# Low parts of a chunk's products and down weights made in the middle of a five-instruction split on GpSimd

## The chip, the cores and the metric

The kernel runs on one NeuronCore of a Trainium2 chip. The metric is the device time of one execution in microseconds (us), the median over several executions. The engines are TensorE (PE in the profile; its weight loads PEld), VectorE (DVE), ScalarE (ACT), GpSimd (POOL) and SyncE (SP, which here only issues DMAs). Each engine works through its own list of instructions in order; they meet through semaphores.

## The reference, cut to what matters

```python
xn = layernorm(x)                                    # x: 8 x 256 tokens x 128
qkv = xn @ Wqkv + bqkv                               # 16 heads of width 8
q = q * cos + rotate_half(q) * sin                   # k in the same way
probs = softmax(q @ k.T / sqrt(8));  attn = (probs @ v) @ Wout + bout
s = sigmoid(xn @ gate_w + gate_b)                    # 16 experts
values, experts = top_k(s, 2);  values /= values.sum()
mlp(x, wg, wu, wd) = (silu(x @ wg) * (x @ wu)) @ wd  # inner width 64
ffn = xn + mlp(xn, shared) + sum(values * mlp(xn, experts))
out = x + attn + ffn
```

Everything is computed in full for every expert; the routing weights, zero for all but two experts of a token, multiply the products before the down projection.

## The kernel before, in words

The 8 sequences are worked in 4 groups of two (512 token columns a group). Two streams of work are woven into each other by a hand-written order of **blocks** from -6 to 33. All engines run the same loop over the blocks, each doing its share of a block.

**The expert stream.** The shared MLP and the 16 experts make 9 chunks a group (the shared one with 64 rows, then two experts a chunk with 128), 36 in all. Block b starts chunk n = b + 6 and carries on with chunk m = b + 5. For a chunk, PE makes the up products in the banks FA and FB (three matmuls each: high weights times high input, low times high, high times low, lines 374 to 376). ACT takes the tanh (`th`, L673), DVE forms `th` (L895) and the product `gu` (L876). GpSimd multiplies `gu` by the routing weights `wbc` (L986). ACT writes the rounded high part `hid_hi` (L694), GpSimd the low part `hid_lo` = `gu` - `hid_hi` (L1002), and PE multiplies both by the down weights into the bank Y, one block later. The down weights have a low part `wd_lo` too, which GpSimd makes chunk by chunk while m is below 9 (L969). The weights `wbc` of a chunk come by two DMAs issued by SP (`load_route`, L336) ahead of their use.

**The attention stream.** The rotated q and k of a sequence are split into three bfloat16 parts by five dependent instructions (`split_stage`): stage 0 adds the two halves of the rotation (L253), stage 1 casts part 0 (L257), stage 2 takes the rest (L259), stage 3 casts part 1 (L261), stage 4 makes part 2 (L262). There are 14 such splits on GpSimd (in the blocks of the table `SPLIT_BLOCK`); the first is in block -6, where no chunk is yet under way, and the others in -5, -2, -1, 0, 2, 6, 7, 9, 10, 14, 16, 17 and 18. When both splits of a sequence are done, SP writes the parts to DRAM (six DMAs, `scratch`, L303) and reads them back in another layout (`load_hats`, L318, into `q_hat` and `k_hat`). PE makes scores for the row maxima from them (S1, L487), DVE reduces these (`mx`, L886), GpSimd splits the maxima (`md`, L947 to L951), and four blocks after the first scores PE makes the scores again with the maxima in extra rows (S2, L501). ACT exponentiates them (`probs`, L661), and PE multiplies by the values (PV, L515), which waits for all four exponentials of the block before.

**The order on each queue around the change.** SP's list is fixed: the parts and hats of sequence 0, two `wbc` chunks, the parts and hats of sequence 1, then from block -6 on the rest, beginning with the `wbc` of the third, fourth and fifth chunk with a routing weight that is not loaded yet. ACT's order in a block is: exponential 0; tanh, exponential 1 and the copies of other banks; exponential 2, then `hid_hi`; and where a new group starts, the copies `xT_hi` and `xT` of the transposed input (L592, L595) before exponential 3. GpSimd's order in a block is: the maxima (`md`), `gu`, `xT_lo` (the low part of a new group's input, L961), the residual (L957), the split of this block, `wd_lo`, `hid_lo`, and the final sum (L1010).

The lines that the change touches are `split_batch` and its call in GpSimd's loop.

Of the kernel before, what the change touches and what calls it, by code (L numbers as in the profile page):

```python
# [33 lines left out]
CHLEAD = 6  # L34
ROUTE_STAGES = 7
SPLIT_STAGES = 5
PART_STAGES = (1, 3, 4)
FIRST, LAST = -CHLEAD, NBLK + 1

# [21 lines left out]
SPLIT_BLOCK = {  # L61
# [4 lines left out]
}  # L66
# [13 lines left out]
def early_b(blk):  # L80

    return [(kind, of) for kind, blocks in EARLY_B.items() for of, at in blocks.items() if at == blk]


def negated_half(blk):

    return blk // 2 + 1 if blk % 2 == 0 and blk // 2 + 1 in range(2 * B) else None
# [20 lines left out]
def bank_uses():  # L108

    a = {("G1", 0): 0, ("G2a", 0): 1, ("G3a", 0): 2}  # L110
    b = {("G2b", 0): 0, ("G3b", 0): 1, ("G4b", 0): 2}
    s = {}
    for blk in range(FIRST, LAST + 1):
        n, q = blk + CHLEAD, blk + LEAD
        if n < NCHUNKS:
            a["hg", n] = len(a)
        for what in late_a(blk):
            a[what] = len(a)
        for what in early_b(blk):
            b[what] = len(b)  # L120
        if n < NCHUNKS:
            b["hu", n] = len(b)
        for i in range(NQ):
            if 0 <= q < NBLK:
                s["max", q * NQ + i] = len(s)
            if i == 0 and transposed_half(blk) is not None:
                s["M", transposed_half(blk)] = len(s)
    return a, b, s


def layer_kernel(nc, x, wqk, wv, bias, wout, gate_w, gate_b, swg, swu, swd, ewg, ewu, ewd,
# [5 lines left out]
    A_USE, B_USE, S_USE = bank_uses()  # L137
# [7 lines left out]
    with ctx:  # L145
# [6 lines left out]
        def sem(name):  # L152
            return ctx.enter_context(nc.semaphore(name))
# [55 lines left out]
        stage = wbc[:, 1].rearrange("p c t -> p (c t)")  # L209
# [23 lines left out]
        fa_ready, fa_read, fb_ready, fb_read = sem("fa_ready"), sem("fa_read"), sem("fb_ready"), sem("fb_read")  # L233
# [6 lines left out]
        def chunk_group(n):  # L240
            return n // NCH, n % NCH
# [5 lines left out]
        def split_stage(engine, queue, stage, w, g, slot):  # L247


            cols = slice(slot * T, (slot + 1) * T)  # L250
            whole, left, part = rope[:, w, 0, cols], rest[:, w, cols], [parts[:, w, k, cols] for k in range(PARTS)]
            if stage == 0:
                return engine.tensor_tensor(whole, whole, rope[:, w, 1, cols], ALU.add)  # L253
            if stage == 1:
                if g:
                    queue.wait_ge(scratch_done[slot], 16 * WRITES * g)
                return engine.tensor_scalar(part[0], whole, 1.0, 1.0, ALU.mult, ALU.mult)  # L257
            if stage == 2:
                return engine.tensor_tensor(left, whole, part[0], ALU.subtract)  # L259
            if stage == 3:  # L260
                return engine.tensor_scalar(part[1], left, 1.0, 1.0, ALU.mult, ALU.mult)  # L261
            return engine.tensor_tensor(part[2], left, part[1], ALU.subtract)  # L262
# [642 lines left out]
        def _(pool):  # L905
            steps = [0]

            def after(instruction):

                steps[0] += 1  # L910
                instruction.then_inc(pool_step, 1)
                pool.wait_ge(pool_step, steps[0])
# [9 lines left out]
            for k, (w, hi, lo) in enumerate(((wg_sb, wg_hi, wg_lo), (wu_sb, wu_hi, wu_lo))):  # L922
                pool.wait_ge(up_hi_ready, k + 1)
                nc.gpsimd.tensor_tensor(lo[:], w, hi[:].bitcast(f32), ALU.subtract).then_inc(up_split, 1)
            def split_batch(w, g, slot):
                kind = ("G2", "G3")[w]
                pool.wait_ge(fa_read, A_USE[kind + "a", g] + 1)
                pool.wait_ge(fb_read, B_USE[kind + "b", g] + 1)
                for stage in range(SPLIT_STAGES):
                    instruction = split_stage(nc.gpsimd, pool, stage, w, g, slot)  # L930
                    if stage not in PART_STAGES:
                        after(instruction)
                        continue
                    instruction.then_inc(parts_done[slot], 1)
                    if stage < SPLIT_STAGES - 1:
                        pool.wait_ge(parts_done[slot], PARTS * (2 * g + w) + PART_STAGES.index(stage) + 1)

# [35 lines left out]
            for blk in range(FIRST, LAST + 1):  # L973
                n = blk + CHLEAD
                m = n - 1
                if negated_half(blk) is not None:
                    negate_maxima(negated_half(blk))
                if 0 <= m < NCHUNKS:
                    g, c = chunk_group(m)
                    pool.wait_ge(fb_read, B_USE["hu", m] + 1)  # L980
                    if c == 0:
                        nc.gpsimd.tensor_scalar(gu[0:I, m % 2, :], gu[0:I, m % 2, :], 0.5, 1.0,
                                                ALU.mult, ALU.mult).then_inc(gu_weighted, 1)
                    else:
                        pool.wait_ge(wbc_ld[c - 1], 32 * (g + 1))
                        nc.gpsimd.tensor_tensor(gu[:, m % 2, :], gu[:, m % 2, :], wbc[:, g % 2, c - 1, :],  # L986
                                                ALU.mult).then_inc(gu_weighted, 1)
                for kind, g in late_a(blk):
                    if kind == "G1":
                        xt_low(g)  # L990
                for g in range(G):
                    if blk == RESIDUAL_BLOCK[g]:
                        residual(g)
                for (g, w, slot), at in SPLIT_BLOCK.items():
                    if blk == at:
                        split_batch(w, g, slot)
                if 0 <= m < NCH:
                    down_low(m)
                if 0 <= m < NCHUNKS:
                    rows = I if m % NCH == 0 else P  # L1000
                    pool.wait_ge(hid_hi_ready, m + 1)
                    nc.gpsimd.tensor_tensor(hid_lo[0:rows, m % 2, :], gu[0:rows, m % 2, :],  # L1002
                                            hid_hi[0:rows, m % 2, :].bitcast(f32), ALU.subtract).then_inc(hid_ready, 1)
                for kind, g in early_b(blk):
                    if kind == "O2":
                        pool.wait_ge(fb_read, B_USE[kind, g] + 1)
                        flat = resid[:, g % 2].rearrange("p t c -> p (t c)")

                        pool.wait_ge(fa_read, A_USE["O1", min(GB * g + 1, B - 2)] + 1)
                        nc.gpsimd.tensor_tensor(flat, flat, y_tok[:], ALU.add).then_inc(o_ready, 1)  # L1010
# [61 lines left out]
```

## Time and profile before

| | us |
|---|---|
| median of the runs | 248.81 |
| lowest and highest of 3 runs | 248.80, 249.73 |
| the profiled execution | 249.88 |
| its span, from the first to the last instruction | 248.1 |
| PE busy in the span | 215.0 |
| DVE busy | 182.7 |
| POOL busy | 174.3 |
| ACT busy | 141.9 |

The profiled execution is 1.07 us above the median. Busy time is a sum over stages with different limits; which engine sets the pace has to be read from each stretch of the trace. Times in the rows below are from the start of the span.

### The profile page before, as it was taken

The numbers are of one execution on the slowest core, as the hardware profiler recorded it, in microseconds if no ns is written. First come the engines' busy times: TensorE is split into PE (matmuls) and PEld (weight loads), VectorE is DVE, ScalarE is ACT, GpSimd is POOL, SyncE is SP. The second block draws the span as 40 slices with busy tenths as digits, with TensorE's granted clock in tenths as the row PEclk, the third lists the DMA queues.
The fourth block names the chain that finished last, engine by engine and source line by source line (L and its number), as shares of the span: only waits on it lengthen the run. The fifth ranks groups of instructions, "written<-read, shape, count | busy, mean of one in ns | idle before, by whom it ended". The sixth has DMA issues, their size and how long they took to land.

```text
span 248.1 us, 4856 instructions
## 1 busy us (share of the span) xinstructions
PE 215.0 (87%) x1612; PEld 140.9 (57%) x1612; DVE 182.7 (74%) x400; ACT 141.9 (57%) x266; POOL 174.3 (70%) x254
## 2 busy tenths in 40 slices
PE   0474399869798999999998999999999999999973
PEld 0342255546465566666674566666766667675541
DVE  5987349958777687999976787998688878774301
ACT  2554322314565766676567476666676767667761
POOL 9184297599998757996966577879886774658622
PEclk9997769979999999999999999999999999999999
DMA  7925344520160276130565150405524640311101
GB/s 223 366 45 168 95 145 139 169 88 0 46 180 21 80 196 155 44 106 10 154 193 166 50 148 26 124 5 174 153 64 127 194 141 19 82 56 35 44 3 42
DMA packets 35954, 26.53 MB, mean 107 GB/s; under 512 B 4237, under 2 KB 30157, under 8 KB 35917
## 3 DMA queue, kind: packets, MB, share of 16 engines
q1 hardware_dynamic: 35224, 25.30, 34.4%
q10 hardware_dynamic: 704, 0.92, 1.0%
q8 instruction: 13, 0.21, 0.4%
q14 instruction: 13, 0.10, 0.1%
HBM read 18.53 MB, written 7.47 MB: 105 GB/s over the span
## 4 chain that ended last, share of the span: by engine, by line
PE 52%; POOL 19%; DVE 11%; issue 6%; DMA 4%; ACT 4%; SPq 3%; POOLq 0%; DVEq 0%; ACTq 0%
PE PV L515 9%; PE S2b L501 5%; POOL hid_lo L1002 4%; PE S2a L501 4%; PE S1a L487 3%; PE S1b L487 3%; POOL gu L986 3%; PE Y L374 3%; PE FB L374 3%; PE FB L376 2%; PE FB L375 2%; PE FA L374 2%; PE Y L375 2%; PE Y L376 2%; PE FA L376 2%
## 5 line engine op out<-in xcount | busy, mean ns | idle before, releaser
L1002 POOL TENSOR_TENSOR hid_lo<-gu,hid_hi 128x512 fp32r<-128x512 f32 (+1 forms) x36 | 46.1, 1281 | 25.5 <-ACT hid_hi L694 25.5
L661 ACT ACTIVATE probs<-S2b 128x512 f32<-128x512 f32 x64 | 38.2, 596 | 30.1 <-PE S2b L501 29.9
L886 DVE TENSOR_REDUCE mx<-S1a 128x2 f32<-128x512 f32 x65 | 44.4, 684 | 10.4 <-PE S1a L487 10.4
L886 DVE TENSOR_REDUCE mx<-S1b 128x2 f32<-128x512 f32 x63 | 43.0, 683 | 7.7 <-PE S1b L487 7.6
L661 ACT ACTIVATE probs<-S2a 128x512 f32<-128x512 f32 x64 | 38.4, 599 | 12.7 <-PE S2a L501 10.6
L986 POOL TENSOR_TENSOR gu<-gu,wbc 128x512 f32<-128x512 f32 x32 | 41.1, 1285 | 6.0 <-DVE gu L876 4.2
L515 PE MATMUL PV<-probs,vx 128*32 128x256 f32 x512 | 34.9, 384 | 1.7 <-ACT probs L661 1.7
L694 ACT ACTIVATE hid_hi<-gu 128x512 fp32r<-128x512 f32 (+1 forms) x36 | 22.7, 632 | 21.3 <-POOL gu L986 19.4
L895 DVE SCALAR_TENSOR_TENSOR th<-th,FA 128x512 f32<-128x512 f32 (+1 forms) x36 | 24.6, 682 | 10.8 <-ACT th L673 10.2
L673 ACT ACTIVATE th<-FA 128x512 f32<-128x512 f32 (+1 forms) x36 | 21.5, 598 | 17.0 <-PE FA L376 16.6
L876 DVE TENSOR_TENSOR gu<-FB,th 128x512 f32<-128x512 f32 (+1 forms) x36 | 24.6, 683 | 8.4 <-PE FB L376 8.3
L487 PE MATMUL S1a<-k_hat,q_hat 96*128 96x256 bf16 x130 | 25.3, 275 | 1.1 <-DVE mx L886 1.1
L501 PE MATMUL S2a<-q_hat,k_hat 102*128 102x256 bf16 x128 | 24.9, 276 | 0.2 <-ACT probs L661 0.2
L501 PE MATMUL S2b<-q_hat,k_hat 102*128 102x256 bf16 x128 | 25.0, 277 | 0.0
L487 PE MATMUL S1b<-k_hat,q_hat 96*128 96x256 bf16 x126 | 24.5, 275 | 0.4 <-DVE mx L886 0.2
L515 PEld LDWEIGHTS PV<-probs,vx 128*32 128x32 f32 x512 | 15.6, 109 | 11.8 <-ACT probs L661 6.9
L374 PE MATMUL Y<-hid_hi,wd_hi 128*128 128x512 f32 (+1 forms) x36 | 17.7, 492 | 4.3 <-POOL hid_lo L1002 4.3
L374 PE MATMUL FB<-xT_hi,wu_hi 128*128 128x512 f32 (+1 forms) x36 | 17.7, 492 | 3.8 <-ACT sig L613 3.6
L501 PEld LDWEIGHTS S2b<-q_hat,k_hat 102*128 102x128 bf16 x128 | 8.6, 98 | 18.1 <-issue 15.9
L374 PE MATMUL FA<-xT_hi,wg_hi 128*128 128x512 f32 (+1 forms) x36 | 17.6, 488 | 1.1 <-ACT xT L595 0.9
L501 PEld LDWEIGHTS S2a<-q_hat,k_hat 102*128 102x128 bf16 x128 | 9.5, 98 | 11.1 <-issue 7.1
L487 PEld LDWEIGHTS S1a<-k_hat,q_hat 96*128 96x128 bf16 x130 | 11.9, 99 | 5.4 <-DVE mx L886 2.5
(129 smaller groups left out, 435.3 us busy)
## 6 DMA issues: line engine op xcount, KB each, us to landing
wbc<-route_w SPq DMA_DIRECT2D x64, 128.0 KB, 3.0
q_hat<-q_parts SPq DMA_DIRECT2D x32, 96.0 KB, 2.6
k_hat<-k_parts SPq DMA_DIRECT2D x32, 96.0 KB, 2.7
k_parts<-parts SPq DMA_DIRECT2D x8, 192.0 KB, 2.1
q_parts<-parts SPq DMA_DIRECT2D x8, 192.0 KB, 2.2
x_sb<-in_x SPq DMA_DIRECT2D x4, 256.0 KB, 4.1
q_parts<-parts SPq DMA_DIRECT2D x8, 128.0 KB, 2.1
k_parts<-parts SPq DMA_DIRECT2D x8, 128.0 KB, 2.1
```

The source lines that it names most:

```text
L374: nc.tensor.matmul(bank, w_hi, m_hi, start=start, stop=False)
L487: last = nc.tensor.matmul(bank[:, t * T:(t + 1) * T], q_hat[0:MROW, slot, pair, t * P:(t + 1) * P], k_hat[0:MROW, slot, pair, r, :], start ...
L501: last = nc.tensor.matmul(S2[head % 2][:, s * T:(s + 1) * T], k_hat[0:KALL, slot, pair, r, s * P:(s + 1) * P], q_hat[0:KALL, slot, pair, : ...
L515: last = nc.tensor.matmul(PV[32 * j:32 * j + 32, hg * T:(hg + 1) * T], vx[:, (b // GB) % 2, SB * (b % GB) + s, r, NQ * hg + j, :], probs[: ...
L661: nc.scalar.activation(probs[:, head % (2 * NQ), :], S2[head % 2][:], ACT.Exp, scale=SCALE).then_inc(exp_done, 1)
L673: nc.scalar.activation(th[0:rows, n % 2, :], FA[0:rows, :], ACT.Tanh, scale=0.5).then_inc(th_ready, 1)
L694: nc.scalar.activation(hid_hi[0:rows, (n - 1) % 2, :], gu[0:rows, (n - 1) % 2, :], ACT.Copy).then_inc(hid_hi_ready, 1)
L876: nc.vector.tensor_tensor(gu[0:rows, m % 2, :], FB[0:rows, :], th[0:rows, m % 2, :], ALU.mult).then_inc(fb_read, 1)
L886: nc.vector.tensor_reduce(mx[:, (q // QB) % 2, (q // 2) % 2, :, q % 2, i], S1[use % 2][:].rearrange("p (t s) -> p t s", t=SB), axis=AX.X, ...
L895: nc.vector.scalar_tensor_tensor(th[0:rows, n % 2, :], th[0:rows, n % 2, :], 1.0, FA[0:rows, :], ALU.add, ALU.mult).then_inc(fa_read, 1)
L986: nc.gpsimd.tensor_tensor(gu[:, m % 2, :], gu[:, m % 2, :], wbc[:, g % 2, c - 1, :], ALU.mult).then_inc(gu_weighted, 1)
L1002: nc.gpsimd.tensor_tensor(hid_lo[0:rows, m % 2, :], gu[0:rows, m % 2, :], hid_hi[0:rows, m % 2, :].bitcast(f32), ALU.subtract).then_inc(hi ...
```

## The change

A split's five instructions are no longer issued in one piece. `split_batch` takes a first and an end stage and is called twice in a block: once for stages 0 and 1 where the whole split stood, and once for stages 2 to 4 behind `wd_lo` and `hid_lo`. The waits for the split's inputs stay in front of stage 0. The wait for stage 1 to be done, which stage 2 needs, stays behind stage 1 and so now stands in front of `wd_lo` or `hid_lo`.

```diff
+SPLIT_PAUSE = 2
...
-            def split_batch(w, g, slot):
+            def split_batch(w, g, slot, first, end):
                 kind = ("G2", "G3")[w]
-                pool.wait_ge(fa_read, A_USE[kind + "a", g] + 1)
-                pool.wait_ge(fb_read, B_USE[kind + "b", g] + 1)
-                for stage in range(SPLIT_STAGES):
+                if first == 0:
+                    pool.wait_ge(fa_read, A_USE[kind + "a", g] + 1)
+                    pool.wait_ge(fb_read, B_USE[kind + "b", g] + 1)
+                for stage in range(first, end):
                     instruction = split_stage(nc.gpsimd, pool, stage, w, g, slot)
...
                 for (g, w, slot), at in SPLIT_BLOCK.items():
                     if blk == at:
-                        split_batch(w, g, slot)
+                        split_batch(w, g, slot, 0, SPLIT_PAUSE)
                 if 0 <= m < NCH:
                     down_low(m)
                 if 0 <= m < NCHUNKS:
...
                     nc.gpsimd.tensor_tensor(hid_lo[0:rows, m % 2, :], gu[0:rows, m % 2, :],
                                             hid_hi[0:rows, m % 2, :].bitcast(f32), ALU.subtract).then_inc(hid_ready, 1)
+                for (g, w, slot), at in SPLIT_BLOCK.items():
+                    if blk == at:
+                        split_batch(w, g, slot, SPLIT_PAUSE, SPLIT_STAGES)
```

The number of instructions is the same on every engine (257 rows on GpSimd in both), and no other engine's list changes. Line numbers of the changed kernel are one or two higher here than in the kernel before.

On GpSimd in block -5, the second split, which completes sequence 1, with the first chunk (m = 0). Before:

```order
L961 TENSOR_TENSOR xT_lo<-xT,xT_hi 128x512
L253 TENSOR_TENSOR rope<-rope 128x256
L257 TENSOR_SCALAR parts<-rope 128x256
L259 TENSOR_TENSOR rest<-rope,parts 128x256
L261 TENSOR_SCALAR parts<-rest 128x256
L262 TENSOR_TENSOR parts<-rest,parts 128x256
L969 TENSOR_TENSOR wd_lo<-wbc,wd_hi 64x128
L1002 TENSOR_TENSOR hid_lo<-gu,hid_hi 64x512
L986 TENSOR_TENSOR gu<-gu,wbc 128x512
```

The same place in the changed kernel:

```order
L963 TENSOR_TENSOR xT_lo<-xT,xT_hi 128x512
L254 TENSOR_TENSOR rope<-rope 128x256
L258 TENSOR_SCALAR parts<-rope 128x256
L971 TENSOR_TENSOR wd_lo<-wbc,wd_hi 64x128
L1004 TENSOR_TENSOR hid_lo<-gu,hid_hi 64x512
L260 TENSOR_TENSOR rest<-rope,parts 128x256
L262 TENSOR_SCALAR parts<-rest 128x256
L263 TENSOR_TENSOR parts<-rest,parts 128x256
L988 TENSOR_TENSOR gu<-gu,wbc 128x512
```

`wd_lo` and `hid_lo` moved ahead of the last three instructions of the split, and so the last `parts`, for which SP waits, moved behind them; the next `gu` stands where it stood.

On GpSimd in block 0 (chunk m = 5), followed by block 1's `gu`. Before:

```order
L986 TENSOR_TENSOR gu<-gu,wbc 128x512
L253 TENSOR_TENSOR rope<-rope 128x256
L257 TENSOR_SCALAR parts<-rope 128x256
L259 TENSOR_TENSOR rest<-rope,parts 128x256
L261 TENSOR_SCALAR parts<-rest 128x256
L262 TENSOR_TENSOR parts<-rest,parts 128x256
L969 TENSOR_TENSOR wd_lo<-wbc,wd_hi 128x128
L1002 TENSOR_TENSOR hid_lo<-gu,hid_hi 128x512
L986 TENSOR_TENSOR gu<-gu,wbc 128x512
```

The same place in the changed kernel:

```order
L988 TENSOR_TENSOR gu<-gu,wbc 128x512
L254 TENSOR_TENSOR rope<-rope 128x256
L258 TENSOR_SCALAR parts<-rope 128x256
L971 TENSOR_TENSOR wd_lo<-wbc,wd_hi 128x128
L1004 TENSOR_TENSOR hid_lo<-gu,hid_hi 128x512
L260 TENSOR_TENSOR rest<-rope,parts 128x256
L262 TENSOR_SCALAR parts<-rest 128x256
L263 TENSOR_TENSOR parts<-rest,parts 128x256
L988 TENSOR_TENSOR gu<-gu,wbc 128x512
```

Here too `hid_lo` stands three instructions nearer to its own `gu`, and the following `gu` has the same instructions ahead of it as before.

## Rows read from the trace of the kernel before

**Rows 1.** The page: the chain that ended last, share of the span by engine.

```profile
PE 52%; POOL 19%; DVE 11%; issue 6%; DMA 4%; ACT 4%; SPq 3%; POOLq 0%; DVEq 0%; ACTq 0%
```

**Rows 2.** Who waited for whom, whole span: us in total, times, longest.

```profile
PE Y L374 <- POOL hid_lo L1002: 4.3, 4, 2.2
```

**Rows 3.** POOL's timeline in block -5: start, us, engine, line, operation, tiles.

```profile
32.48 0.67 POOL L259 TENSOR_TENSOR rest<-rope,parts 128x256 f32<-128x256 f32 x1
...
33.73 0.67 POOL L262 TENSOR_TENSOR parts<-rest,parts 128x256 bf16<-128x256 f32 x1
34.36 0.45 POOL L969 TENSOR_TENSOR wd_lo<-wbc,wd_hi 64x128 fp32r<-64x128 f32 x1
34.78 1.26 POOL L1002 TENSOR_TENSOR hid_lo<-gu,hid_hi 64x512 fp32r<-64x512 f32 x1
36.00 1.28 POOL L986 TENSOR_TENSOR gu<-gu,wbc 128x512 f32<-128x512 f32 x1
```

**Rows 4.** The chain that ended last, 34 to 47 us: start, us, what.

```profile
34.42 0.35 SPq L303
...
40.15 1.37 SPq L318
...
44.00 2.86 DMA wbc<-route_w
```

**Rows 5.** SP's loads of k_hat: duration ns min/median/max, first and last start us.

```profile
L318 SPq DMA_DIRECT2D k_hat<-k_parts x32: 333/443/1372, 22.6 to 203.1; - x32
```

**Rows 6.** POOL's timeline, block -2: start, us, and idle before with its releaser.

```profile
47.00 1.29 POOL L986 TENSOR_TENSOR gu<-gu,wbc 128x512 f32<-128x512 f32 x1 [1.77 <-DMA wbc<-route_w]
...
49.56 0.68 POOL L259 TENSOR_TENSOR rest<-rope,parts 128x256 f32<-128x256 f32 x1
```

**Rows 7.** Busy time by stretch: us, then PE, PEld, DVE, ACT, POOL (instructions), clock, DMA, GB/s.

```profile
47.00:79.00 32.00, 26.05 (x180) 16.75 (x179) 25.43 (x61) 14.83 (x28) 29.95 (x47) 0.95 0.26 77
88.00:111.00 23.00, 23.00 (x186) 15.47 (x185) 19.88 (x49) 14.61 (x29) 18.24 (x30) 1.00 0.45 123
```

**Rows 8.** PE's timeline: its three long waits for `hid_lo`, and the Y of chunk 8.

```profile
53.19 0.79 PE L374 MATMUL Y<-hid_hi,wd_hi 128*128 128x512 f32 x1 [2.22 <-POOL hid_lo L1002]
...
66.89 0.50 PE L374 MATMUL Y<-hid_hi,wd_hi 128*128 128x512 f32 x1 [1.17 <-POOL hid_lo L1002]
...
78.61 0.50 PE L374 MATMUL Y<-hid_hi,wd_hi 128*128 128x512 f32 x1 [0.77 <-POOL hid_lo L1002]
...
84.65 0.48 PE L374 MATMUL Y<-hid_hi,wd_hi 128*128 128x512 f32 x1
```

**Rows 9.** ACT's timeline: `hid_hi` of chunks 5 and 8.

```profile
61.98 0.63 ACT L694 ACTIVATE hid_hi<-gu 128x512 fp32r<-128x512 f32 x1 [1.92 <-POOL gu L986]
...
79.83 0.63 ACT L694 ACTIVATE hid_hi<-gu 128x512 fp32r<-128x512 f32 x1 [1.58 <-POOL gu L986]
```

**Rows 10.** POOL's timeline at the end of its full stretch (chunk 8).

```profile
78.53 1.28 POOL L986 TENSOR_TENSOR gu<-gu,wbc 128x512 f32<-128x512 f32 x1
81.51 1.29 POOL L961 TENSOR_TENSOR xT_lo<-xT,xT_hi 128x512 fp32r<-128x512 f32 x1 [1.71 <-ACT xT L595]
...
83.18 1.28 POOL L1002 TENSOR_TENSOR hid_lo<-gu,hid_hi 128x512 fp32r<-128x512 f32 x1
```

**Rows 11.** SP's timeline: the first DMAs behind the parts of sequence 2.

```profile
70.42 1.10 SPq L336 DMA_DIRECT2D wbc<-route_w  x2
```

**Rows 12.** Block 17: ACT's `hid_hi` and POOL's stage 2.

```profile
167.41 0.62 ACT L694 ACTIVATE hid_hi<-gu 128x512 fp32r<-128x512 f32 x1
167.44 0.67 POOL L259 TENSOR_TENSOR rest<-rope,parts 128x256 f32<-128x256 f32 x1
```

**Rows 13.** DVE's and POOL's timelines in block 16: two instructions on `wsel`, and `hid_lo`.

```profile
161.26 0.29 DVE L778 TENSOR_TENSOR wsel<-iota_sb,topf 128x128 f32<-128x128 f32 x1
162.53 1.29 POOL L1002 TENSOR_TENSOR hid_lo<-gu,hid_hi 128x512 fp32r<-128x512 f32 x1
162.65 1.32 DVE L783 TENSOR_TENSOR wsel<-wsel,tsel 128x128 f32<-128x128 f32 x1
```

## The prediction, made before the changed kernel ran

> **What bounds the kernel now.** I read the chain that ended last first. It is 52% PE, but 19% POOL [rows 1], so the question is where POOL's part lies. Followed in order of time, the chain goes through POOL's second split to 34.4 us, through SP's queue and DMAs to 47 [rows 4], through POOL again to 78.6, and from there mostly through PE to the end. The table of busy time says the same: from 47 to 79 us POOL is busy 29.95 of 32 us, the rest being short pauses between dependent instructions, and PE only 26.05; from 88 to 111 us PE is busy 23.00 of 23 and POOL 18.24 [rows 7]. So there are three stages: a start-up that hangs on SP's list, a stretch in which POOL is the bottleneck, and a long rest in which PE is. Two waits matter then. PE waits for `hid_lo` 4.3 us in four places [rows 2]; three lie in the POOL stretch, 2.22, 1.17 and 0.77 us [rows 8], which leaves 0.14 for the fourth. And POOL itself starts its full stretch late, because the `gu` at 47.00 had to wait 1.77 us for the DMA of its routing weights [rows 6].
>
> **What the change moves.** No instruction is added or taken away. In 13 blocks `hid_lo`, in the early ones with `wd_lo` ahead of it, stands in front of split stages 2 to 4. Two prices follow, both from start-to-start distances.
> `hid_lo` is released earlier by the three stages: 34.36 - 32.48 = 1.88 us [rows 3].
> The last part of the split, for which SP waits, comes later by `wd_lo` and `hid_lo`: 36.00 - 34.36 = 1.64 us [rows 3].
> The `gu` of the next block has the same work ahead of it as before and keeps its time, unless POOL now has to stand still for `hid_hi`.
>
> **Block -5, a loss on the path.** SP starts the six writes of sequence 1's parts at 34.42, right behind POOL's last part (33.73 + 0.67) [rows 3, 4]. Now `wd_lo` starts in stage 2's place at 32.48, `hid_lo` at 32.90, stage 2 at 34.12, and the last part is done at 34.40 + 1.64 = 36.04. Everything behind it in SP's list moves by 1.64 us: six writes and their landing, eight hat loads, and then the `wbc` DMA issued at 44.00 that takes 2.86 us [rows 4]. That one releases the `gu` at 47.00 [rows 6], the first instruction of POOL's full stretch. The `gu` had idled until then, so nothing hides the delay: it starts at 48.64. What `hid_lo` gains in block -5 buys nothing, since its Y is not one of the four that wait.
>
> **Blocks -2 to 3, the POOL stretch.** I see no input that would come too late for POOL, so it works on from 48.64 without a break, as from 47.00 before. `hid_hi` starts 79.83 - 78.53 = 1.30 us behind the start of its `gu` and takes 0.63 [rows 9, 10]; the new `hid_lo` stands 49.56 - 47.00 + 0.42 = 2.98 us behind it [rows 3, 6]. So every `gu` is 1.64 us late, up to the one at 78.53, which comes at 80.17.
> On PE's side the earlier `hid_lo` cancels this, and a little more: 1.64 - 1.88 = -0.24 us at each of the three waits. Y comes at about 52.9, 66.6 and 78.4. If that were all, the kernel would be no slower.
> But PE has a second tie to POOL, and the change does not loosen it. In ACT's list `hid_hi` stands in front of the last exponential of a block, and `hid_hi` waits for `gu`: 1.92 us at 61.98, 1.58 at 79.83 [rows 9]. Those exponentials are all 1.64 us late, and PE's PV products need them. So PE saves 0.24 us at a Y and loses up to 1.6 at the next PV. In block 3, which has no split to gain from, it is worst: the late `gu` makes `hid_hi`, `xT`, `xT_lo` (81.51) and `hid_lo` late by the same 1.64, and `hid_lo` ends at 83.18 + 1.28 + 1.64 = 86.10 [rows 9, 10]. The Y that started at 84.65 [rows 8], 0.2 us behind its `hid_lo`, cannot start before. PE is **1.4 us late**, and from here on PE is the bottleneck [rows 7], with nothing idle that could take the delay back.
>
> **SP's list again.** In block 0 the parts of sequence 2 come later by both shifts, 1.64 + 1.64 = 3.3 us. Behind them stand the `wbc` of chunk 8 and the hats of sequence 2. Those `wbc` loads were issued at 70.42, over 1.10 us [rows 11]; at 73.7 + 1.1 + 2.86 they land by 77.7, 2.5 us before the `gu` at 80.17. I take nothing for this.
>
> **Blocks 6 to 18, stalls of POOL.** Eight splits lie where PE is the bottleneck. There `hid_hi` can be later than stage 2 was: in block 17 it ends at 168.03 where stage 2 began at 167.44, so POOL stands still 0.59 us [rows 12], with stages 2 to 4, the maxima and the next `gu` queued behind it. That is the largest of the eight; two are zero. POOL has 4.8 us to spare in 23 [rows 7], so these do not add up. I take 0.1 us, with 0 and 0.6 (one stall that gets through) as ends. The gain there is at most the 0.14 us of PE's fourth wait.
>
> **Sum.** 1.4 + 0.1 - 0.1 = +1.4 us on the profiled execution's 249.88, which gives 251.3. That execution is 1.07 us above the median; carried to the median of 248.81 it is **250.2 us**.
>
> **A rule weighed.** Of two DVE instructions of one size, the one at 161.26 took 0.29 us and the one at 162.65 took 1.32: it had begun while POOL's `hid_lo` ran from 162.53 to 163.82 [rows 13]. The Trainium skill (SBUF — State Buffer, "SBUF: two separate sides") says that GpSimd and a VectorE instruction with two SBUF inputs hold a port pair as an exclusive lock, and that the loser waits for the winner's whole instruction; the row agrees. By that rule the moved `hid_lo` frees such an instruction in one block and may block one in another, up to a microsecond either way on the sum.
>
> **The rivals.**
> *Absorbed (no change).* The 1.64 us do not reach 47 us in full. In SP's list the hat load at 40.15 took 1.37 us where the median is 0.44 [rows 4, 5]. If that pause belongs to the time and not to the place in the list, 0.9 us are saved: +0.5, or 249.3. For it: the pause is a single one. Against it: all that stands around it is a chain, each link of which moves.
> *Faster.* PE's waits for `hid_lo` set the end, and the exponentials do not. The first wait is shortened by 1.88, the others vanish: 1.88 + 1.17 + 0.77 + 0.14 = 4.0 us, or 244.8; with the start-up delay of 1.64 against it, 246.5. It is decided at the PV products: if these had room of over 1.6 us behind their exponentials, this case would win. Against it speak POOL's 29.95 of 32 busy us: reordering a full engine does not take a delay out of it.
> *More than forecast.* A stall for `hid_hi`, or a DVE instruction held up for the 1.32 - 0.29 = 1.03 us of rows 13, reaches PE once or twice on top of the 1.4: +2.4 to +3.4, or 251.2 to 252.2. The same exchange may also give back as much.
> *That the change does not do what it says* is excluded; GpSimd's list shows it in 13 blocks.
>
> **How the numbers follow.** A difference of 0.5% (1.24 us) is about what a measurement of this kernel can tell from no change. Forecast case (+1.0 to +1.9): 0.62, of which 0.47 lies above 1.24 and 0.15 below. Absorbed (-1.0 to +1.0): 0.17. Faster: 0.08. More: 0.13. That makes slower 0.47 + 0.13 = 0.60, same 0.15 + 0.17 = 0.32, faster 0.08. The range reaches down through most of the absorbed case, to 248.6, and up to one late stall with its scatter, 251.7; outside are the faster case and half of the one above.
>
> **What would show it.** In the changed kernel's trace: SP's first L303 of sequence 1 at about 36.1 instead of 34.4; the `gu` that waits for the DMA at 48.6 instead of 47.0, after a wait of some 3.4 instead of 1.77 us; POOL full from there to 80; PE's waits for `hid_lo` at Y near 52.9, 66.6 and 78.4; new waits of PE for ACT's `probs` ahead of PV products in that stretch, and one of over 1 us for `hid_lo` near 86; POOL's waits for `hid_hi` up by 1 to 2.5 us in blocks 6 to 17. It would be wrong if the `gu` came at 47.0 as before, or if PE reached block 5 less than 1 us late.

## The result, and the profile after

The changed kernel takes 252.53 us (median of 4 runs, 252.35 to 252.95), the kernel before 248.81 in the same comparison (4 runs, 248.71 to 249.73): a ratio of 1.0144 (95% interval 1.0116 to 1.0171), slower. The forecast was slower, by the right mechanism, but 250.2 with a range up to 251.7. The loss was 3.7 us where 1.4 had been forecast. A second comparison of the same two kernels, with the kernel before in 27 runs and the changed one in 9, gave 1.0109 (1.0074 to 1.0145), or 2.7 us. The profiled executions span 250.7 and 248.1 us, 2.6 apart.

The chain that ended last, of the changed kernel: by engine, and in order of time from GpSimd's split in block -5 (start, us, what). It answers to [rows 1] and [rows 4].

```profile
PE 52%; POOL 16%; DVE 12%; DMA 6%; issue 6%; ACT 4%; SPq 3%; POOLq 0%; ACTq 0%; DVEq 0%
...
32.50 0.45 POOL wd_lo L971
32.95 1.24 POOL hid_lo L1004
34.19 0.64 POOL rest L260
34.91 0.40 POOL parts L262
35.40 0.68 POOL parts L263
36.09 0.35 SPq L304
...
38.56 3.03 DMA k_parts<-parts
41.61 0.33 SPq L319
...
45.87 2.86 DMA wbc<-route_w
```

`wd_lo` and `hid_lo` now stand in the chain itself, ahead of the last part. SP's first write begins at 36.09 instead of 34.42. Two links behind it differ from the rows of before. The last write takes 3.03 us to land, where it had taken 1.90 in the kernel before. And none of the hat loads on the chain takes the 1.37 us of [rows 5]; all are at 0.33 to 0.45.

GpSimd's timeline in block -5 and at the `gu` of chunks 3 and 8, and PE's and ACT's waits behind it (columns as in [rows 6]), of the changed kernel:

```profile
34.16 0.66 POOL L260 TENSOR_TENSOR rest<-rope,parts 128x256 f32<-128x256 f32 x1
35.40 0.67 POOL L263 TENSOR_TENSOR parts<-rest,parts 128x256 bf16<-128x256 f32 x1
...
48.87 1.27 POOL L988 TENSOR_TENSOR gu<-gu,wbc 128x512 f32<-128x512 f32 x1 [4.84 <-DMA wbc<-route_w]
...
80.16 1.28 POOL L988 TENSOR_TENSOR gu<-gu,wbc 128x512 f32<-128x512 f32 x1
```

```profile
53.14 0.59 PE L375 MATMUL Y<-hid_hi,wd_hi 128*128 128x512 f32 x1 [3.36 <-POOL hid_lo L1004]
...
60.42 0.39 PE L488 MATMUL S1b<-k_hat,q_hat 96*128 96x256 bf16 x2 [1.07 <-DVE mx L887]
...
65.19 0.27 PE L477 MATMUL S1a<-identb_sb,md 128*24 128x128 bf16 x2 [1.18 <-DVE mx L887]
...
70.93 1.07 PE L516 MATMUL PV<-probs,vx 128*32 128x256 f32 x16 [0.55 <-ACT probs L662]
...
83.12 0.50 PE L375 MATMUL FA<-xT_hi,wg_hi 128*128 128x512 f32 x1 [1.52 <-ACT xT L596]
...
86.28 0.48 PE L375 MATMUL Y<-hid_hi,wd_hi 128*128 128x512 f32 x1
```

```profile
63.65 0.63 ACT L695 ACTIVATE hid_hi<-gu 128x512 fp32r<-128x512 f32 x1 [3.37 <-POOL gu L988]
```

The `gu` of chunk 3 is 1.87 us later than in [rows 6], and the `gu` of chunk 8 is 1.63 later than in [rows 10]. The wait in front of the first is 4.84 us where about 3.4 had been forecast: GpSimd was through with its work in front of it at 44.03 instead of 45.23, which bought nothing, since the load was to come. (In `only_m5`, with the same pause, it was at 45.1; why it was sooner in `after` is not shown.) PE's Y in block -2 starts at 53.14 where [rows 8] have 53.19: the earlier `hid_lo` cancels the delay at that place, as forecast. But PE is late elsewhere, and the Y of chunk 8 comes at 86.28 instead of 84.65.

Who waited for whom, and busy time by stretch, of the changed kernel (columns as in [rows 2] and [rows 7]):

```profile
ACT hid_hi L695 <- POOL gu L988: 29.9, 14, 6.1
...
POOL hid_lo L1004 <- ACT hid_hi L695: 28.7, 25, 2.8
...
DVE th L896 <- ACT th L674: 15.3, 19, 2.7
```

```profile
47.00:79.00 32.00, 24.89 (x173) 16.02 (x172) 26.10 (x58) 14.06 (x28) 28.20 (x44) 0.95 0.28 87
88.00:111.00 23.00, 22.39 (x180) 14.63 (x178) 19.59 (x45) 14.55 (x27) 16.36 (x27) 1.00 0.51 141
```

POOL did 28.20 us of work between 47 and 79 instead of 29.95, because its full stretch begins 1.87 us later. PE did 24.89 instead of 26.05. PE's own waits for `hid_lo` fell from 4.3 us to 3.4, all of it in one place, and that bought nothing.

### The profile page after: what moved, and what is told of

The parts are those of the page before. It is cut to its first block, busy times and chain, and to the rows that moved or that the text cites. A ratio compares the mean times of both kernels' runs of the same rounds, so it can differ in the third digit from the quotient of the medians.

```text
span 250.7 us, 4865 instructions
## 1 busy us (share of the span) xinstructions
PE 214.8 (86%) x1612; PEld 140.9 (56%) x1612; DVE 186.7 (74%) x400; ACT 140.7 (56%) x266; POOL 173.7 (69%) x254
## 4 chain that ended last, share of the span: by engine, by line
PE 52%; POOL 16%; DVE 12%; DMA 6%; issue 6%; ACT 4%; SPq 3%; POOLq 0%; ACTq 0%; DVEq 0%
PE PV L516 10%; PE S2b L502 5%; PE S2a L502 4%; PE S1a L488 4%; POOL hid_lo L1004 3%; PE S1b L488 3%; POOL gu L988 3%; PE FA L375 3%; PE FA L377 2%; PE FA L376 2%; PE FB L375 2%; DVE mx L887 2%; PE Y L375 2%; PE FB L376 2%; PE FB L377 2%
## 5 line engine op out<-in xcount | busy, mean ns | idle before, releaser
L896 DVE SCALAR_TENSOR_TENSOR th<-th,FA 128x512 f32<-128x512 f32 (+1 forms) x36 | 24.6, 683 | 15.9 <-ACT th L674 15.3
```

Of the source, the lines that this page charges most:

```text
L896: nc.vector.scalar_tensor_tensor(th[0:rows, n % 2, :], th[0:rows, n % 2, :], 1.0, FA[0:rows, :], ALU.add, ALU.mult).then_inc(fa_read, 1)
```

## The experiments

Seventeen traces are read by four times: the start of the `gu` of chunk 3 (the end of the start-up), of the `gu` of chunk 8 (the end of POOL's full stretch), of the last `gu`, and the span. This table is worked out from GpSimd's timelines; the ratios are to the kernel before, run beside them (4 runs for `after`, 19 to 31 for the others). The kernel itself had 10 runs where no other number stands behind its interval.

```
                    gu 3   gu 8   8 minus 3   last - gu 8   span    ratio  [95%]
before             47.00  78.53     31.53       154.81     248.1
after              48.87  80.16     31.29       155.85     250.7   1.0144 [1.0116, 1.0171] (4)
before_again       46.99  78.26     31.27       154.60     247.6   1.0012 [0.9986, 1.0038] (12)
after_again        49.37  80.51     31.14       154.69     249.9   1.0109 [1.0074, 1.0145] (9)
only_m5            49.51  80.80     31.29       155.52     251.1   1.0102 [1.0065, 1.0139] (7)
all_but_m5         46.17  77.45     31.28       155.36     247.5   1.0002 [0.9974, 1.0030] (12)
only_late          46.99  78.34     31.35       155.15     248.2   0.9990 [0.9962, 1.0018]
m5_wd_only         46.92  78.23     31.31       155.61     248.6   1.0012 [0.9970, 1.0054]
m5_hid_first       49.89  81.15     31.26       153.98     249.9   1.0117 [1.0041, 1.0192] (4)
only_m5_again      48.12  79.39     31.27       154.61     248.7   1.0096 [1.0062, 1.0129] (9)
before_hh          45.50  76.84     31.34       157.29     248.1   1.0056 [1.0034, 1.0079]
all_but_m5_hh      45.90  77.21     31.31       158.06     249.2   1.0045 [1.0006, 1.0085]
before_wbc2        45.09  76.47     31.38       154.85     246.0   0.9959 [0.9932, 0.9986]
after_wbc2         45.30  77.16     31.86       154.61     246.5   0.9957 [0.9928, 0.9986]
before_resid       46.43  76.87     30.44       154.23     245.8   0.9991 [0.9955, 1.0027]
before_wbc2_resid  45.05  75.47     30.42       155.83     246.5   0.9929 [0.9899, 0.9958]
after_wbc2_resid   44.63  75.59     30.96       154.96     245.3   0.9921 [0.9891, 0.9952]
```

### Which of the 13 blocks costs the time

The two kernels first, once more and unchanged.

> The kernel before, unchanged, as its own control. The changed kernel's median is 3.72 us above the one before, but its profiled span is only 2.6 us longer (250.7 against 248.1), and the profiled execution of before (249.88) lay 1.07 us above its median. If that execution was an odd one, this run's time is near 248.8, its span near 247.0, and the trace shows where the first one lost about 1 us. If the traces are typical and something outside the span differs, the span is 248.1 again at a time of 248.8. Ratio 1.000, within 0.002.

> The changed kernel, unchanged, on the same chip as the partial ones: 252.5 us, +3.7 on before, if the measured difference is the kernel's own; the trace should again show the gu that waits for its routing weights at 48.9 and PE waiting 0.6 us for the rows of maxima near 96 us. If that 0.6 us was an accident of the DMA queue, it is gone and the span is 250.1.

They took 249.57 and 252.05 us, 0.8 above and 0.5 below what they had been, and so 2.5 apart. The 3.7 us expected of the pair did not come back. A wait of PE for a DMA, 0.60 us at 96.22 in `after`, was gone in `after_again`. Their traces make the cleanest pair: the `gu` of chunk 3 is 2.38 us later, the `gu` of chunk 8 is 2.25 later, the span is 2.3 longer. From chunk 8 to the last `gu` the two differ by 0.1.

Then the change in block -5 alone, and in all the others.

```diff
 SPLIT_STAGES = 5
+SPLIT_PAUSE = 2
+PAUSED = (-5,)
...
-                        split_batch(w, g, slot)
+                        split_batch(w, g, slot, 0, SPLIT_PAUSE if blk in PAUSED else SPLIT_STAGES)
...
+                for (g, w, slot), at in SPLIT_BLOCK.items():
+                    if blk == at and blk in PAUSED:
+                        split_batch(w, g, slot, SPLIT_PAUSE, SPLIT_STAGES)
```

> Only block -5 has the split paused; the other twelve blocks are as before. Start-up theory (the last parts of sequence 1 are late, SP's whole list with them): the gu at 47.0 comes at 48.7 to 48.9, PE's waits for hid_lo are as before at positions 1.7 us later, and the loss is the whole 3.7 us or a little more, 252.3 to 253.0. Rival (the pauses in the twelve later blocks cost time of their own, through POOL standing still for hid_hi): only 1.6 us here, 250.4.

> The split is paused in all blocks but -5. Start-up theory: the gu is back at 47.0 and nearly nothing is lost, 248.5 to 249.3; hid_lo comes 1.9 us earlier at the Ys of the POOL stretch, but the exponentials behind hid_hi hold PE, so no gain above 0.3 us. Rival (later blocks): 2.0 us of the loss stays, 250.9.

The other twelve blocks are the same edit with `PAUSED = (-2, -1, 0, 2, 6, 7, 9, 10, 14, 16, 17, 18)`; the eight late ones, with `PAUSED = (6, 7, 9, 10, 14, 16, 17, 18)`, are the third kernel.

> The split is paused only in blocks 6 to 18, where PE is the bottleneck. The trace of the variant without block -5 showed a shift against before of -1.1 us up to chunk 11 and of -0.5 at the end, so these eight blocks should cost about 0.5 us: 249.3 to 249.8. If the cost comes from the early blocks' changed phase instead, it is 0.

Block -5 alone gives 252.24 us, the whole loss of the second comparison; its `gu` of chunk 3 came at 49.51, later than the 48.7 to 48.9 expected. The other twelve give 249.25, a ratio of 1.0002, and the eight late ones 248.96 or 0.9990, below the 249.3 to 249.8 that had been expected of them. Twelve of the 13 moves are therefore worth nothing either way, although without block -5 they do what they were made for. PE's waits of `all_but_m5` in and behind the POOL stretch:

```profile
54.79 0.50 PE L376 MATMUL FA<-xT_hi,wg_hi 128*128 128x512 f32 x1 [0.95 <-ACT vx L604]
...
62.37 1.07 PE L517 MATMUL PV<-probs,vx 128*32 128x256 f32 x16 [1.70 <-ACT probs L663]
...
68.35 1.07 PE L517 MATMUL PV<-probs,vx 128*32 128x256 f32 x16 [0.91 <-ACT probs L663]
...
80.42 0.50 PE L376 MATMUL FA<-xT_hi,wg_hi 128*128 128x512 f32 x1 [1.14 <-ACT xT L597]
```

No wait for `hid_lo` is left in that stretch: the 2.22, 1.17 and 0.77 us of [rows 8] are gone. In their place PE waits for exponentials (`probs`) and for ACT's copies out of the bank FA (`vx`, `xT`). The forecast named this second tie.

### Lateness or interruption

The loss in block -5 could come from the last part being late, or from the split being interrupted. Two kernels tell these apart. One pauses the split for `wd_lo` alone (+0.42 us). The other doesn't pause it, but puts `wd_lo` and `hid_lo` ahead of all five stages, so that the last part is as late as in the change and the stages stay together (its edit is shown against that of block -5 alone). The third is block -5 of the change once more, beside them.

```diff
-                if first == 0:
+                if first == 0 and end:
...
-                        split_batch(w, g, slot, 0, SPLIT_PAUSE if blk in PAUSED else SPLIT_STAGES)
+                        split_batch(w, g, slot, 0, 0 if blk in PAUSED else SPLIT_STAGES)
...
                 for (g, w, slot), at in SPLIT_BLOCK.items():
                     if blk == at and blk in PAUSED:
-                        split_batch(w, g, slot, SPLIT_PAUSE, SPLIT_STAGES)
+                        split_batch(w, g, slot, 0, SPLIT_STAGES)
```

> In block -5 alone, wd_lo stands ahead of stages 2 to 4 and hid_lo behind them; all else as before. The last parts are 0.42 us late instead of 1.64. If the loss follows the lateness, SP's first write is at 34.8 and the gu that waits for its routing weights 0.4 to 0.5 us later than before's 46.2 to 47.0, 249.3 to 249.6 in time. If the excess over 1.64 us in the changed kernel comes from the writes' landing meeting a packet of instructions near 38.5 to 40 us, the landing is still 1.9 us here, since the writes end at about 39.2.

> In block -5 alone, wd_lo and hid_lo stand ahead of the whole split, which is in one piece. The last parts are as late as in the changed kernel (1.64 us), with no pause. If lateness is all, it costs what the pause in block -5 alone did: 251.3 to 252.0 (ratio near 1.010), with the gu at 48.6 to 49.5. If the pause itself costs something, it costs less: 250.6.

> The pause in block -5 alone once more, to see whether the landing of the last write (3.34 us in the first look, 1.9 in every kernel with the split in one piece) is long again. A landing of 3.0 to 3.4 with an instruction packet in the same stretch and a time of 251.5 would make the excess over 1.64 us part of what the change does; a landing of 1.9 and a gu at 48.0 to 48.6 would make it chance.

With `wd_lo` alone the ratio is 1.0012, inside the scatter (249.76 us, a little over the 249.3 to 249.6 expected), and the last write landed in 1.90 us. With both ahead and no interruption it is 1.0117, from four runs and with a wide interval, beside 1.0096 for the pause; its time of 252.26 us and its `gu` at 49.89 lie above what had been expected. A split interrupted but hardly late costs nothing that can be seen, and a late one costs the same without interruption. The interruption is not the cause; the last part's lateness is. GpSimd's `gu` of chunk 3 in `m5_hid_first`, and one piece of its chain, the landing of the last write:

```profile
49.89 1.26 POOL L989 TENSOR_TENSOR gu<-gu,wbc 128x512 f32<-128x512 f32 x1 [5.45 <-DMA wbc<-route_w]
```

```profile
38.67 3.60 DMA k_parts<-parts
```

### Is it the order of SP's list

If the path runs over SP's list, it must help to issue the two `wbc` loads ahead of the writes that wait for the split. Two pairs of loads move up.

```diff
             load_route(0, 1)
+            load_route(0, 2)
+            load_route(0, 3)
             scratch(1)
...
-                if 2 < ahead < NCHUNKS and ahead % NCH:
+                if 4 < ahead < NCHUNKS and ahead % NCH:
```

> The kernel before, with one edit in SP's list: the routing weights of the third and fourth chunk (wbc 2 and 3) are loaded ahead of the parts and hats of sequence 1, while SP idles for those parts, instead of behind them. Start-up theory: the gu at 47.0 no longer waits for a DMA and starts behind the maxima at 45.2 to 45.5; all that follows moves by 1.5 us and the time is 1.3 to 1.8 us below before (ratio 0.994). Rival (the POOL stretch has another input that is just in time): nothing is gained.

> The changed kernel with the same edit of SP's list. Start-up theory: the late parts of sequence 1 no longer stand in front of the routing weights, so the gu starts at 45.2 to 45.5 here too, and the changed kernel loses its start-up loss of 1.9 us and the wait of before: within 0.8 us of before_wbc2, about 248.0 (0 to 0.8 us more for the later blocks). Rival (the twelve later blocks carry the loss): 2 us or more above before_wbc2.

The `gu` of chunk 3, of the kernel before and of the changed one with this edit:

```profile
45.09 1.29 POOL L988 TENSOR_TENSOR gu<-gu,wbc 128x512 f32<-128x512 f32 x1
```

```profile
45.30 1.28 POOL L990 TENSOR_TENSOR gu<-gu,wbc 128x512 f32<-128x512 f32 x1
```

Neither waits for a DMA any more, and the two kernels take the same time: 248.17 and 248.33 us, ratios 0.9959 and 0.9957. The difference of 1.1% between them is gone with the one link. This also makes the kernel before faster, but by less than the `gu` gains: 1.91 us there, 1.0 by the ratio. Of the 1.91, 0.9 are the long hat load of the one trace `before`; against the 46.17 of `all_but_m5`, which has none, the `gu` gains 1.1. Of PE's waits for `hid_lo` in `before_wbc2` this one is the longest, the same as the second of [rows 8]:

```profile
64.84 0.50 PE L376 MATMUL Y<-hid_hi,wd_hi 128*128 128x512 f32 x1 [1.18 <-POOL hid_lo L1004]
```

### What else ties PE to GpSimd

The forecast said that the exponentials behind `hid_hi` in ACT's list tie PE to GpSimd's `gu`. Putting `hid_hi` behind the last exponential of a block takes that tie away.

```diff
-                    if i == 2 and 0 <= n - 1 < NCHUNKS:
+                    if i == 3 and 0 <= n - 1 < NCHUNKS:
```

> The kernel before, with ACT's hid_hi moved behind the last exponential of its block (and behind xT_hi and xT). It tests the second tie of PE to POOL: if the exponentials behind hid_hi hold PE in the POOL stretch, PE's waits for probs go away there, but in the kernel before its waits for hid_lo remain (4 us) and POOL is full, so the time changes by less than 0.5 us there; xT_lo no longer waits 1.7 us near 81.5, which can give 1 us. Expected 247.8 to 248.9. In the late stretch hid_hi comes later by one exponential; if POOL's queue suffers from that, the time is above 249.5.

> The split paused in all blocks but -5, and ACT's hid_hi behind the last exponential. The faster rival said that the earlier hid_lo (1.9 us) would pay if the exponentials did not hold PE. Here they do not. If that is the only tie, this kernel is 1 us or more below before_hh, whose median was 250.6. If POOL's full stretch is the reason by itself (the Y of chunk 8, in a block without a split, comes when POOL is through), it is within 0.5 us of before_hh, 250.1 to 251.0, and the waits of PE for hid_lo at the first Ys are gone while one near 84 appears.

Expected was a gain of 0.2 to 1.3 us for `before_hh`; it lost 1.4 (249.11 to 250.56). The start-up was even 1.5 us shorter (0.9 of it the long hat load of `before`), and the full stretch the same (31.34 us), but from chunk 8 to the last `gu` it took 157.29 us, and 158.06 in `all_but_m5_hh`, where all others have 153.98 to 155.85. So the move costs some 2.5 us where PE is the bottleneck. With the twelve pauses the kernel loses the same (250.50), so even with the exponentials ahead of `hid_hi` the earlier `hid_lo` gains nothing. PE's S1b from 88 to 240 us, of the kernel before and then of `before_hh` (busy us, mean ns, and the idle time ahead with its releaser):

```profile
L487 PE MATMUL S1b<-k_hat,q_hat 96*128 96x256 bf16 x90 | 17.3, 272 | 0.2 <-DVE mx L886 0.2
```

```profile
L487 PE MATMUL S1b<-k_hat,q_hat 96*128 96x256 bf16 x90 | 17.3, 272 | 1.7 <-DVE mx L886 1.7
```

1.5 us of the loss show as PE's waits for DVE's `mx`. Which link makes `mx` late there was not followed. This experiment does not show the tie to be worthless in the early stretch; it shows that this way to cut it costs more than it gives. What the tie alone costs stays open.

Last, POOL's stretch itself. The residual of group 0, an instruction of GpSimd in block 1, moves to block -6, where GpSimd has room.

```diff
-RESIDUAL_BLOCK = (1, 8, 22, 23)
+RESIDUAL_BLOCK = (-6, 8, 22, 23)
```

> The kernel before, with the first group's residual (L957, 1.25 us on POOL) made in block -6, where POOL idles, instead of block 1, in POOL's full stretch. If POOL sets the pace from 47 to 79 us, every gu from chunk 7 on comes 1.25 us earlier and the time falls by 1.0 to 1.3 us (ratio 0.995 to 0.996), though no wait of PE for it stood in the profile. If PE sets the pace and POOL only looks full, nothing changes.

> Both edits of the start and the POOL stretch on the kernel before: SP's list (gu at 45.1 instead of 47.0) and the residual. The two add up if they act on one chain: 2.0 + 1.25 us of span, about 246.0 to 246.8 (ratio 0.989 to 0.991).

> The changed kernel with the same two edits. As with the SP edit alone it should stand within 0.5 us of its twin with the whole split; 246.3 to 247.2. Were the pause worth its 1.9 us once PE is nearer to being the bottleneck in that stretch, it would be 1 us below its twin.

The stretch is shortened from 31.3 to 30.4 us, by 0.9 of the 1.25 that the instruction had taken from start to start (68.03 to 69.28 in `before`). The missing 0.3 us came back as a wait of GpSimd for ACT's `hid_hi`, in front of the `hid_lo` right behind the gap; of `before_resid`:

```profile
68.08 1.29 POOL L1002 TENSOR_TENSOR hid_lo<-gu,hid_hi 128x512 fp32r<-128x512 f32 x1 [0.32 <-ACT hid_hi L694]
```

So another engine stands close behind GpSimd in this stretch. In time, alone it gave 0.9991, where 1.0 to 1.3 us less had been expected and no difference is shown, and with the wbc edit 0.9929 and 0.9921, short of the 0.989 to 0.991 expected of the first. These two beat both kernels: 247.76 and 247.10 us, 1.2 to 1.9 us below the 249.0 of the kernel before beside them. Between them the pauses show no clear difference: the one with them is 0.7 us faster by the medians, and the intervals overlap.

## Why the prediction was right or wrong

**Right: the path in block -5.** The forecast moved SP's first write to about 36.1, and it came at 36.09; it named every link behind it and said that nothing there hides a delay. From that write to the `gu` of chunk 3 it is 11.64 to 11.67 us in all 13 traces with SP's list in its old order, once what the last write's landing took over 1.90, a hat load over its usual 0.44 (0.39 for one of the eight) and the `wbc` load over 2.86 is taken off. `only_m5` has the whole loss, `m5_hid_first` has it without any interruption, and the wbc edit takes it away in both kernels. This part is shown.

**Wrong in size: the step "it starts at 48.64".** The forecast let the 1.64 us travel through SP's list to the `gu` with every link as long as before. Five traces with the late part have that `gu` at 48.87, 49.37, 49.51, 49.89 and 48.12, mean 49.15. Four with the part in its old place (`before`, `before_again`, `only_late`, `all_but_m5`) have it at 47.00, 46.99, 46.99 and 46.17, mean 46.79. That is 2.4 us, not 1.64. The first write itself is at 36.13 and 34.49 in the mean, and these are the 1.64. The other 0.7 lie in the three links named above, which took 0.5 to 2.0 us over their usual time in the five late traces and 0.1 to 1.0 in the four early ones. The "absorbed" rival saw that the hat's 1.37 us need not move along, and that came true: with no such pause in `after`, 0.9 us were saved. But I priced it as a gain and held the writes' landing for rigid. It took 3.03 us in `after`, 3.25 in `after_again`, 3.34 in `only_m5` and 3.60 in `m5_hid_first`, where the traces with the early part have 1.9. Between 1.1 and 1.7 us went there. The fifth shows the other case. `only_m5_again` is the same program as `only_m5`; in its profiled execution the landing took 1.90 us, the `gu` came at 48.12, and the time was 250.56, 1.5 us below the median of its own runs. By what had been written down for it ahead of the run, this makes the excess chance, and not a fixed part of the change; four of the five late traces have it all the same, and none of the early ones. From its chain:

```profile
38.44 1.90 DMA k_parts<-parts
...
45.11 2.87 DMA wbc<-route_w
```

**Why the landing is long: an association.** The DMA engines of the changed kernel from 38 to 39 us, while the last write is under way (queues: packets, MB, share of 16 engines; then issues, with us to landing):

```profile
q1 hardware_dynamic: 564, 0.27, 93.0%
q8 instruction: 1, 0.02, 7.5%
...
q_parts<-parts SPq DMA_DIRECT2D x1, 192.0 KB, 2.3
k_parts<-parts SPq DMA_DIRECT2D x1, 64.0 KB, 3.0
```

One packet of the queue that the profile names `instruction` lies among the writes' data; 7.5% of 16 engines' microsecond is 1.2 us of one engine. The busy share of the DMA engines from 36 to 46 us, in 40 slices, of the changed kernel and of `all_but_m5`:

```profile
DMA  0001719989989988100000000038487858576748
```

```profile
DMA  9999999984000005667675768666785265586674
```

In the first the bulk of the writes is done near 40.0 and SP goes on only at 41.61; in the second, which has no such packet there, SP goes on where the bulk ends. In every trace with a landing of 3.0 us or more the packet lay in the writes' stretch. In `before`, `before_again` and `only_m5_again` it lay behind the writes, among the hats, and there a hat load took 1.37, 0.99 and 0.87 us instead of its usual time. In `only_late` it lay at 44.0, in the time of the `wbc` load, which took 3.84 us instead of 2.86. Where there was none among writes or hats, neither was slow. No run moved the packet by itself: that it causes the delay is the reading that fits, not shown. Why it lies at 39 to 40 us in one execution of a program (`only_m5`) and at 41 to 42 in the next (`only_m5_again`) stays open.

**Right, and sharper than I had it: the full stretch is rigid.** From chunk 3 to chunk 8 GpSimd takes 31.14 to 31.53 us in 13 of the 14 traces whose stretch holds the same work, late or early, paused or not. `after_wbc2` stands out with 31.86, and so does its twin without the residual, 30.96 against 30.4. In `after_wbc2` the five small instructions of one set of maxima, from 57.47 us on, took 1.83 us from first start to the next `gu` instead of 1.36 in `before_wbc2`; what held them is not shown. A delay at its start comes out at its end: +1.87 in and +1.63 out. That `hid_lo` comes 1.88 us earlier inside it does nothing for the end, as forecast. Nor is the clock a term of it. Busy time from 50 to 62 us, of `only_m5` and of `all_but_m5` (columns as in [rows 7]):

```profile
50.00:62.00 12.00, 6.96 (x34) 5.02 (x32) 6.08 (x21) 3.86 (x8) 11.23 (x18) 0.72 0.24 63
```

```profile
50.00:62.00 12.00, 9.44 (x55) 5.99 (x53) 10.65 (x35) 4.13 (x9) 11.06 (x20) 1.00 0.16 45
```

In the first PE stood idle 4.82 us ahead of a Y, and its granted clock was at 1.2 GHz for about half of these 12 us (mean 0.72); in the second it stayed at 2.4. The stretch took 31.29 and 31.28 us.

**Right in kind, wrong in place: PE's second tie.** I expected waits for `hid_lo` at 52.9, 66.6 and 78.4 and one over 1 us near 86. Only the first came (53.14, 3.36 us, longer since PE arrived early). The others were overtaken by waits for `mx` at 60.42 and 65.19 and for `probs` at 70.93. The one for `probs` is the tie that I had named; ACT's `hid_hi` also holds up the `th` behind it, and DVE's wait for `th` rose from 10.2 to 15.3 us. The two for `mx` have another source. DVE works without a pause from 56.75 us past 65, and two of its small instructions in that time were slow in the changed kernel:

```profile
57.95 1.22 DVE L769 TENSOR_TENSOR den<-top 128x4 f32<-128x4 f32 x1
...
62.52 1.25 DVE L784 TENSOR_TENSOR wsel<-wsel,tsel 128x128 f32<-128x128 f32 x1
```

In the kernel before they took 0.18 and 0.77. GpSimd's `hid_lo` ran from 57.86 and its `gu` from 62.34, 1.28 us each: this is the delay of [rows 13], and it did reach PE, but in a stretch whose end GpSimd sets. `after_again` has both again, with 1.21 and 1.25. The one near 86 came as a wait of 1.52 us for ACT's `xT` at 83.12: FA's bank has that reader, and `xT` is late with all of ACT's list. So the path to chunk 8's Y was not `hid_lo`, whose Y had 0.2 us of room, but this wait for `xT`, which had none: FA came at 83.12 instead of 81.49, and the Y was late by the same 1.63 us where I had 1.4.

**Right: nothing from the late blocks and from the block-0 list.** GpSimd's waits for `hid_hi` rose by 3.2 us over the whole span (the forecast said 1 to 2.5 for the late blocks; `only_late` has 3.0 more), and the time of `only_late` did not move. The hats and `wbc` behind block 0 show as no wait of GpSimd: its `gu` at 80.16 has none. The lock of rows 13 had stood as a cause for up to 1 us either way. In `only_m5` an instruction of DVE that took 0.26 us in the kernel before took 1.31, in step with a `hid_lo` of GpSimd:

```profile
113.21 1.31 DVE L773 CAST topf<-topi 128x8 f32<-128x8 uint32 x1
```

```profile
113.21 1.29 POOL L1005 TENSOR_TENSOR hid_lo<-gu,hid_hi 128x512 fp32r<-128x512 f32 x1
```

The order of GpSimd's work is the kernel before's from block -4 on there, so the collision comes from a shift in time alone. Such hits move with the relative time of the two engines. The time from chunk 8 to the last `gu` spreads by some 1.9 us (153.98 to 155.85), without a sign that belongs to the pauses; how much of it these hits make is not shown. The Trainium skill (SBUF — State Buffer, "SBUF: two separate sides") gives the exclusive lock for VectorE instructions in a 2-port performance mode or with two SBUF inputs. The cast has one input; whether it ran in such a mode no run here shows, so its row neither bears out the rule nor speaks against it.

**Wrong: the sum, and the room above.** Two terms were off. The sum took 1.07 us off to get from the profiled execution to the median. That held for the kernel before alone: the profiled execution of `after` took 252.58 us, 0.05 above its median. Between the two profiled executions the loss is 2.7 us where 1.4 was forecast; the other 1.0 of the 2.3 that I missed is this term. The other is the start. With the start as measured, 0.8 us later than forecast, the same sum gives 2.2 us in place of 1.4. The four kernels with the late part in the later comparisons have ratios of 1.0096 to 1.0117, which is 2.4 to 2.9 us of 249. So the mis-sized start is most of what the forecast missed of the later comparisons; 0.2 to 0.7 us more are inside the intervals. Put on 248.81, these ratios give 251.2 to 251.7, the edge of my range. The range had been made from the bounds of my terms, and none of them stood for the scatter of executions: the kernel before alone ran from 247.84 to 251.17 us in 27 runs. The first comparison's 3.7 us is above all the others. It is four runs each, and its median of the kernel before, 248.81, is the lowest of all (249.00 to 249.21 in the later sets). What its last 0.8 to 1.3 us are stays open. The rival "more than forecast" had a size near it, but by a stall of GpSimd or a hit on DVE that reaches the end, and neither is seen to make it.

## What to carry to other kernels

When an instruction moves back in an engine's list, look first at who waits for it, a DMA queue with an ordered list above all: the delay (1.64 us here) is handed on to everything behind the wait, here to a load that had nothing to do with it. Inside the stretch in which GpSimd was full, changing the order shortened nothing; its start, and work taken out of it, moved its end, and the latter by 0.9 us for 1.25. And the cheap repair is the list: issue what the next stage needs ahead of what waits.

## What was not expected of the hardware

The profile counts packets of a queue `instruction` on the same 16 DMA engines as the data (13 packets with 0.21 MB, so 16 KB each). One took 1.2 us of one engine, and where it fell into the kernel's writes the landing of the last was 3.0 to 3.9 us instead of 1.9 (an association, as told above). Two executions of one program (`only_m5`) had it 2 us apart. A DMA's time in one trace is therefore not a constant to carry over, and neither is the distance of one profiled execution from the median.
